# A two-layer graph network on one core: part of the gathered rows fetched by other engines than GpSimd, and nodes normalised once

## What is computed

```python
edge_index = jnp.stack([src, dst])
h = jnp.maximum(_layernorm(x, axis=-1), 0.0)
# layer 0
agg = jax.ops.segment_sum(h[src], dst, num_segments=N_NODES)
x = x + (agg @ W_rel.T + b_rel + h @ W_root.T)
h = jnp.maximum(_layernorm(x, axis=-1), 0.0)
# layer 1
edge_weights = jax.nn.silu(edge_features @ We1 + be1) @ We2 + be2
agg = jax.ops.segment_sum(h[src] * edge_weights, dst, num_segments=N_NODES)
out = jax.nn.silu(agg @ Wn1 + bn1) @ Wn2 + bn2
x = x + (h + out)
```

## Time and profile before

| | us |
|---|---|
| median of 3 runs | 5621.94 (5613.85 to 5627.18) |
| profiled execution, first to last instruction (span) | 3996.3 |
| POOL busy | 2976.2 (74% of the span) |
| PE matmul busy | 2447.1 |
| DVE busy | 1995.0 |
| ACT busy | 1187.2 |

### The profile page before, as it was taken

One profiled execution on the slowest core, in us unless ns is written; L12 is line 12 of the kernel. 1 busy time (PEld: TensorE's weight loads), 2 busy tenths in 40 slices (PEclk: granted clock), 3 DMA queues, 4 the chain that ended last, 5 costly groups with the idle time before them and its releaser, 6 DMA issues.

```text
span 3996.3 us, 52113 instructions
## 1 busy us (share of the span) xinstructions
PE 2447.1 (61%) x10946; PEld 1882.0 (47%) x10946; DVE 1995.0 (50%) x6931; ACT 1187.2 (30%) x2730; POOL 2976.2 (74%) x3135
## 2 busy tenths in 40 slices
PE   3444444444444444444467788877887777887787
PEld 2334333333433333433445555555555555555555
DVE  6555555555555555555554444444444444444444
ACT  3444444444444444444411111111111111111111
POOL 7777777777777777777567777777777777777776
PEclk8555555555555555555578788788788887888878
DMA  2222222222222222222122222222222222222222
GB/s 84 62 61 61 61 64 67 61 61 61 61 64 67 61 61 61 61 66 64 50 78 78 83 80 79 81 76 83 78 80 82 77 75 83 80 79 82 77 76 82
DMA packets 208083, 284.73 MB, mean 71 GB/s; under 512 B 70338, under 2 KB 137972, under 8 KB 207828
## 3 DMA queue, kind: packets, MB, share of 16 engines
q0 software_dynamic: 100096, 205.20, 18.1%
q1 hardware_dynamic: 66676, 58.00, 4.9%
q10 hardware_dynamic: 41184, 20.45, 1.7%
HBM read 262.97 MB, written 20.45 MB: 71 GB/s over the span
## 4 chain that ended last, share of the span: by engine, by line
POOL 67%; issue 23%; PE 5%; DMA 2%; DVE 1%; POOLq 1%; ACT 0%; SPq 0%; DVEq 0%; ACTq 0%
POOL rows L298 67%; PE hid_ps L368 2%; PE seg_a L330 1%; PE ew_ps L373 1%; DMA rows<-h_rows,idx 1%; PE seg_b L330 1%; DMA ef<-ef_blocks 1%; POOLq L176 1%; POOLq L177 0%; DVE rows L670 0%; DVE onehot L566 0%; DVE ew_ps L666 0%; ACT hidden L502 0%; PE node_t L382 0%; ACT rows L436 0%
## 5 line engine op out<-in xcount | busy, mean ns | idle before, releaser
L298 POOL DMA_INDIRECT rows<-h_rows,idx x1564 | 1490.0, 953 | 522.6 <-issue 515.6
L298 POOL DMA_INDIRECT rows<-x,idx x1564 | 1485.2, 950 | 478.2 <-issue 478.2
L330 PE MATMUL seg_a<-onehot,rows 128*128 128x128 f32 x3312 | 726.6, 388 | 915.0 <-DVE onehot L566 408.1
L330 PEld LDWEIGHTS seg_a<-onehot,rows 128*128 128x128 f32 x3312 | 623.7, 281 | 1148.5 <-issue 960.0
L330 PE MATMUL seg_b<-onehot,rows 128*128 128x128 f32 x2944 | 606.4, 370 | 530.9 <-DVE onehot L566 374.4
L424 ACT ACTIVATE rows<-rows,e_shift,e_rstd 128x128 f32<-128x128 f32 x1564 | 643.3, 481 | 793.0 <-DVE e_shift L593 793.0
L330 PEld LDWEIGHTS seg_b<-onehot,rows 128*128 128x128 f32 x2944 | 520.8, 266 | 727.6 <-issue 448.3
L502 ACT ACTIVATE hidden<-hid_ps,be_col 128x512 f32<-128x512 f32 x391 | 268.8, 687 | 1416.1 <-PE hid_ps L368 1415.8
L373 PE MATMUL ew_ps<-we_sb,hidden 128*128 128x128 f32 x3128 | 539.8, 330 | 49.1 <-ACT hidden L502 49.1
L582 DVE BATCH_NORM_STATS2 e_stats<-rows 128x6 f32<-128x128 f32 x1564 | 339.7, 280 | 426.1 <-DMA rows<-x,idx 361.8
L368 PE MATMUL hid_ps<-ef,we_sb 50*128 50x512 f32 x782 | 522.7, 753 | 39.4 <-DMA ef<-ef_blocks 39.4
(11 more groups left out here) (91 smaller groups left out, 811.5 us busy)
## 6 DMA issues: line engine op xcount, KB each, us to landing
ef<-ef_blocks SPq DMA_DIRECT2D x391, 100.0 KB
rows<-x,idx POOLq DMA_INDIRECT x1564, 2.5
rows<-h_rows,idx POOLq DMA_INDIRECT x1564, 2.5
xs<-x SPq DMA_DIRECT2D x26, 256.0 KB
y_rows<-ys ACTq DMA_DIRECT2D x26, 256.0 KB, 2.5
ys<-y_rows SPq DMA_DIRECT2D x26, 256.0 KB, 3.3
out<-xs ACTq DMA_DIRECT2D x26, 256.0 KB
h_rows<-h1s ACTq DMA_DIRECT2D x24, 256.0 KB, 2.5
```

The costliest lines, as they stand in the source:

```text
L298: pool.indirect_dma_start(out=rows[:, u, t, :], out_offset=None, in_=table, in_offset=bass.IndirectOffsetOnAxis(ap=idx[:, j:j + 1], axis=0 ...
L330: mm = pe.matmul(seg[u % 2][:, 0:P], rows[:, u, t, :], onehot[:, u % 2, t, :], start=(t == 0), stop=(t == TB - 1))
```

## The change

**Nodes once.** Ahead of the edges, the 25 groups of nodes are normalised by a loop of five sets at a time (SP loads `x`, DVE statistics, ACT root and scaling, SP stores to a new `h_rows`). PE transposes each and DVE or ACT (`H_BY_ACT`) copies it into a feature-major table in SBUF: `h_table`, which takes the place of `agg1` while layer 0 runs. POOL does its first iteration from `x` as before, all 68 tiles, and these are normalised by block as before. For iterations 1 to 22 it gathers from `h_rows`; statistics, roots and scaling of edges, and `hs` and its transposes in the node updates, are gone from them. SP's weight loads come earlier.

**Tiles by columns.** In these 22 iterations POOL gathers 62 tiles. Of the other six, three come by ACT and two by DVE: for each edge, one instruction copies the 128x1 column of its source node from the table (`columns`), at a place given by a register. Sixteen row numbers at a time are loaded into registers from `cp_idx` (`indices`). PE transposes the finished 128 columns, and ACT copies them into `rows` (`rows_turned`). The sixth tile comes by 128 transfers of one row each, issued by SP (`bring_rows`). In layer 1 it is four tiles of 68, two by ACT, one by DVE, one by SP, in all 23 iterations; its table `h1_table` (in place of `agg0`) is built between the layers, from `h1_rows`, with loads, transposes and copies of 25 groups. The tiles concerned are the last of an iteration: in layer 0 the last two of block 15 and all of block 16, in layer 1 block 16.

The diff, cut to its core:

```diff
+H_SETS = 5
+assert GROUPS % H_SETS == 0
+CHUNK = 16
+CHUNKS = P // CHUNK
+H_BY_ACT = (3, 4)
+CP_ACT = (3, 2)
+CP_DVE = (2, 1)
+CP_TILES = CP_ACT[0] + CP_DVE[0] + 1
+CP_FIRST = U * TB - CP_TILES
...
+        cp_idx = sb("cp_idx", [ITERS, CP_TILES * P], I32)
+        act_cols, dve_cols = sb("act_cols", [P, 3 * P]), sb("dve_cols", [P, 2 * P])
...
+        h_table, h1_table = agg[1], agg[0]
...
+        def indices(engine, it, first, count):
+
+            row = bass.at_runtime_partition(cp_idx[0:1, first:first + count], it)
+            _, values = nc.values_load_multi_w_load_instructions(
+                row, engines=[engine], min_val=0, max_val=N_NODES - 1,
+                skip_runtime_bounds_check_because="edge sources are node numbers")
+            return values
 
...
+            def load_h(k, r):
+                sp.dma_start(h_x[r], node_group(x, k * H_SETS + r)).then_inc(s_hx[r], 16)
+
+            def store_h(k, r):
+                hold(sp, s_hh, k * H_SETS + (r + 1))
+                sp.dma_start(node_group(h_rows, k * H_SETS + r), h_out[r]).then_inc(s_hstore[r], 16)
+
+            for r in range(H_SETS):
...
+            def bring_rows(table, it, first, count):
+                for n, v in enumerate(indices(mybir.EngineType.SP, it, (CP_TILES - 1) * P + first, count)):
+                    r = first + n
+                    sp.dma_start(rows[r:r + 1, U - 1, TB - 1, :], table[bass.ds(v, 1), :]
+                                 ).then_inc(s_sp_row[r // CHUNK], 16)
...
+                with sp.Fori(1, ITERS) as it:
                     i = p * ITERS + it
                     node_x([loop_group(it)], i)
...
+                    hold(sp, s_seg[0], slot_free(i, U - 1, U))
+                    for c in range(CHUNKS):
+                        bring_rows(h_rows, it, c * CHUNK, CHUNK)
+                        if c == CHUNKS // 2:
+                            rows_landed(0, p, it, 0, HALF)
+                            load_idx(it + 1, 0, HALF, s_idx_a)
+                    rows_landed(0, p, it, HALF, U)
                     load_idx(it + 1, HALF, U, s_idx_b)
+                    tile_brought(0, cp_count(0, p, it))
...
+            ROWS_AT, STEP_ROWS = 4, 10
...
+                        if u == ROWS_AT:
+                            hold(sp, s_seg[1], slot_free(i, U - 1, U))
+                        if u >= ROWS_AT:
+                            first = (u - ROWS_AT) * STEP_ROWS
+                            bring_rows(h1_rows, it, first, min(STEP_ROWS, P - first))
                         if u == HALF + 2:
-                            for v in range(HALF):
-                                hold(sp, s_rows[1][v], i * (16 * TB) + 16 * TB)
+                            rows_landed(1, p, it, 0, HALF)
                             load_idx(it + 1, 0, HALF, s_idx_a)
-                    for v in range(HALF, U):
-                        hold(sp, s_rows[1][v], i * (16 * TB) + 16 * TB)
+                    rows_landed(1, p, it, HALF, U)
                     load_idx(it + 1, HALF, U, s_idx_b)
+                    tile_brought(1, tiles0 + cp_count(1, p, it))
...
+                    for j in range(u * TB, min(u * TB + TB, tiles)):
                         pool.indirect_dma_start(
-                            out=rows[:, u, t, :], out_offset=None, in_=table,
+                            out=rows[:, u, j - u * TB, :], out_offset=None, in_=table,
                             in_offset=bass.IndirectOffsetOnAxis(ap=idx[:, j:j + 1], axis=0),
-                        ).then_inc(s_rows[layer][u], 16)
...
-                    gather(0, x, p * ITERS + it, 0)
+                gather(0, x, p * ITERS, p * ITERS, U * TB, first=True)
+                for r in range(H_SETS):
+                    hold(pool, s_hstore[r], 16 * (GROUPS // H_SETS + 1))
+                with pool.Fori(1, ITERS) as it:
+                    i = p * ITERS + it
+                    gather(0, h_rows, i, i, CP_FIRST)
...
+                    gather(1, h1_rows, i, passes * ITERS + i, (U - 1) * TB)
...
+            def turn_act(layer, n, k):
+                if k == 0:
+                    pe.wait_ge(s_cp_rows[layer], n + 1)
+                pe.wait_ge(s_cp_act[layer], n * CP_ACT[layer] + (k + 1))
+                pe.transpose(cp_ps[:, k * P:(k + 1) * P], act_cols[:, k * P:(k + 1) * P],
+                             ident[:, :]).then_inc(s_act_turn[layer], 1)
+
+            def turn_dve(layer, n, k):
+                out = node_t[0][:, k * P:(k + 1) * P] if layer == 0 else cp_ps[:, CP_ACT[1] * P:(CP_ACT[1] + 1) * P]
+                pe.wait_ge(s_cp_dve[layer], n * CP_DVE[layer] + (k + 1))
...
+                        if u == 6:
+                            turn_act(0, n, 0)
+                        if u == 11:
+                            turn_act(0, n, 1)
+                            turn_dve(0, n, 0)
+                        if u == U - 2:
+                            turn_act(0, n, 2)
+                            turn_dve(0, n, 1)
...
+                        if u < U - 2:
+                            pe.wait_ge(s_rows[0][u], i * (16 * TB) + 16 * TB)
+                        elif u == U - 2:
+                            pe.wait_ge(s_rows[0][u], n * 32 + 32)
+                            pe.wait_ge(s_cp_rows[0], n + 2)
+                        else:
+                            pe.wait_ge(s_sp_tile[0], n + 1)
...
+                        if u == 8:
+                            turn_act(1, i, 0)
+                        if u == U - 2:
+                            turn_act(1, i, 1)
+                            turn_dve(1, i, 0)
...
+                def relu_h(r):
+                    act.wait_ge(s_hshift, k * H_SETS + (r + 1))
+                    act.wait_ge(s_hcopy[r], k + 1)
+                    act.wait_ge(s_hstore[r], k * 16 + 16)
+                    for t in range(TB):
+                        op = nc.scalar.activation(h_out[r][:, t, :], h_x[r][:, t, :], ACT.Relu,
+                                                  bias=e_shift[:, r, t:t + 1], scale=e_rstd[:, r, t:t + 1])
...
+            def columns(layer, table, n, it, c):
+                k, q = c // CHUNKS, c % CHUNKS
+                if q == 0:
+                    act.wait_ge(s_act_turn[layer], n * CP_ACT[layer] + (k + 1))
+                tile = (0, CP_TILES - TB)[layer] + k
+                for e, v in enumerate(indices(mybir.EngineType.Activation, it, tile * P + q * CHUNK, CHUNK)):
+                    at = k * P + q * CHUNK + e
+                    op = nc.scalar.activation(act_cols[:, at:at + 1], table[:, bass.ds(v, 1)], ACT.Copy)
+                if q == CHUNKS - 1:
...
+            def rows_turned(layer, n, i):
+                act.wait_ge(s_act_turn[layer], n * CP_ACT[layer] + 2 * CP_ACT[layer])
+                act.wait_ge(s_dve_turn[layer], n * CP_DVE[layer] + 2 * CP_DVE[layer])
+                act.wait_ge(s_seg[layer], slot_free(i, U - 1, U))
+                if layer == 0:
+                    nc.scalar.activation(rows[:, U - 2, 2:4, :].rearrange("p t f -> p (t f)"),
+                                         cp_ps[:, 0:2 * P], ACT.Copy)
+                    nc.scalar.activation(rows[:, U - 1, 0:1, :].rearrange("p t f -> p (t f)"),
+                                         cp_ps[:, 2 * P:3 * P], ACT.Copy)
+                    nc.scalar.activation(rows[:, U - 1, 1:3, :].rearrange("p t f -> p (t f)"),
+                                         node_t[0][:, 0:2 * P], ACT.Copy).then_inc(s_cp_rows[0], 1)
+                else:
...
+                stats_h(0)
+                for r in range(H_SETS):
+                    if r + 1 < H_SETS:
+                        stats_h(r + 1)
+                    shift_of(r, s_hstd, s_hrecip, s_hshift, k * H_SETS + (r + 1))
+                    if r >= 2:
+                        copy_h(r - 2)
...
+            def columns(layer, table, n, it, c):
+                k, q = c // CHUNKS, c % CHUNKS
+                if q == 0:
+                    dve.wait_ge(s_dve_turn[layer], n * CP_DVE[layer] + (k + 1))
+                tile = (CP_ACT[0], CP_TILES - 2)[layer] + k
+                for e, val in enumerate(indices(mybir.EngineType.DVE, it, tile * P + q * CHUNK, CHUNK)):
+                    at = k * P + q * CHUNK + e
+                    op = v.tensor_copy(dve_cols[:, at:at + 1], table[:, bass.ds(val, 1)])
+                if q == CHUNKS - 1:
...
-                        if u + 1 < U:
-                            edge_shift(i, u + 1)
+                        for c in columns_at(0, u):
+                            columns(0, h_table, cp_count(0, p, it), it, c)
...
+            with dve.Fori(0, GROUPS // H_SETS) as k:
+                for r in range(H_SETS):
+                    if r not in H_BY_ACT:
+                        dve.wait_ge(s_tturn, k * H_SETS + (r + 1))
+                        v.tensor_copy(h1_table[:, bass.ds(k * (H_SETS * BLOCK) + r * BLOCK, BLOCK)],
+                                      h_turn[r][:, :]).then_inc(s_tcopy[r], 1)
...
```

(2 more changed lines are left out.)

360 lines of the change are left out of this document (269 added, 91 removed).

## The result

The changed kernel takes 7319.81 us (7311.54 to 7323.74), the kernel before beside it 5624.56: a ratio of 1.302, 95% interval 1.300 to 1.304. The forecast was 5468 us with a range to 5800, and faster: the sign and the size are both wrong.

What follows compares the result with a forecast made beforehand. POOL's gathers, one every 1.25 us, were taken as the bound, with a DVE and PE chain behind. Start +1, layer 0 -143, late updates -9, between layers +20, layer 1 -23 gave -154: 5468 us, range 5200 to 5800.

Steps and rivals of the forecast that it cites:

- The constant of 1625.6 us: Whole kernel: the median's excess over the profiled span of 3996.3 us, taken to stay the same after the change.
- the rival that spread it over the gathers: POOL in both layers: 0.52 us more for each of 3,128 gathers, gain 397, time 5225 us; chance 0.22.
- Cost 1 us: Nodes' stage at the start: POOL waits for slot 0 until about 96; its second iteration began at 95 before.
- The cover named at 60 us: Start: POOL's first iteration of 68 gathers hides the nodes' stage, worth 60 us if it fails.
- The forecast of DVE's chain: Layer 0: DVE needs 77.5 us an iteration, equal to POOL; 78.5 taken, gain 143 us.
- the 0.35 of the author's estimate: Load of 16 row numbers into registers in one instruction: 0.35 us, near one register's 0.30.
- A block of 3.65 us "becomes 5.6": Layer 1, DVE: a group of columns before the multiply adds 1.9 us to its block.
- PE at the slower pace throughout: Layer 1: upper bound of 89 us an iteration, where 83.3 was summed and 84 taken.
- A second term of layer 1: SP's work with row transfers, row number loads and feature loads: 80 us an iteration, POOL's time.
- Each register costs by itself: Register loads on DVE and ACT: 536 us per us of load, a loss from 0.64 us; chance 0.24.
- Column copies shut POOL out: DVE's column copies block POOL's gathers in both layers: about 1100 us over its gain, 6500 us; chance 0.04.
- POOL stays the bound in both layers: If a DVE column costs 0.10 us or less: gain 278, time 5344 us; chance 0.10.

Runs made afterwards that it cites:

- e1_before: The kernel before, unedited, run again for its trace: 5674.51 us, ratio 1.001.
- e12_best: Changed kernel with columns in layer 0 alone (three tiles ACT, one DVE), no SP rows: 5986.75 us, 1.056 of the kernel before.
- e10_l1_act: Changed kernel with SP's tiles of both layers and DVE's tile of layer 1 back on POOL: 6179.62 us, 1.090 of the kernel before.
- e13_after: The changed kernel, unedited, run again where the kernel before takes 3993 us: 4505.75 us, ratio 1.128.
- e14_columns_0: The kernel of e12_best again, where the kernel before takes 3993 us: 3877.73 us, ratio 0.972.
- e15_l1_act: The kernel of e10_l1_act again, where the kernel before takes 3993 us: 3958.24 us, ratio 0.991.
- e18_cols_after: Changed kernel with DVE's columns of layer 1 moved behind the multiplication: 4294.54 us, ratio 1.076 to the kernel before at 3993 us.
- e5_loop_sp: Kernel before plus extra SP waits in a short loop (4 waits, 6 times) in each block: 4001.08 us, ratio 1.000.
- e3_nodes_once: Changed kernel without columns, SP rows or layer 1 table; nodes normalised once, POOL gathers all tiles: 5614.88 us, 0.993 of the kernel before.
- e2_long_sp: Kernel before plus 34 already-satisfied waits on SP, written out in each of 17 blocks: 6171.43 us, ratio 1.090.
- e4_short_bodies: Changed kernel with fewer tiles moved (layer 0: one each by ACT, DVE, SP; layer 1: one by ACT): 6727.01 us, 1.188 of the kernel before.

## Why the prediction was wrong, step by step

**The constant of 1625.6 us.** This is the step that failed first, and it decides the time on chip A. "I take it as constant", and the rival that spread it over the gathers: both are out. The gathers take 0.95 us on either chip. As far as the rows of e1_before and of the changed kernel show, it is time in which the other engines stand still while POOL gathers, and it is longer in the versions that give these more to do (52, 70, 89 and 114 thousand instructions): 1678 us for the kernel before (5671.51 less 3993.27), 2109 for e12_best (5986.75 less 3877.73), 2221 for e10_l1_act (6179.62 less 3958.24), 2867 for the changed kernel (7372.84 less 4505.75). Of its loss of 1701 us on chip A 512 are there on chip B as well; the other 1189 are this growth, whose cause stays open. A difference between the runs and the trace that is 40% of the trace says that the trace is of another case, not that a constant is missing.

**The model against chip B.** There the same steps can be held to the span of 3996.3 us, for which they were made. By the adds of DVE, before and after (e13_after):

```
                                    before   after   change   forecast
start to first add of iteration 1    116.0   171.7    +55.7         +1
layer 0 from there                  1860.5  1835.8    -24.7       -143
between the layers                    55.5    70.5    +14.9        +11
layer 1                             1951.3  2409.5   +458.2        -23
end                                   12.9    11.4     -1.5          0
span                                3996.3  4498.9   +502.6       -154
```

*The start.* "Cost 1 us" held for POOL, whose second iteration starts at 105.5 (forecast 96). But DVE's first add comes at 105, not 38, and its 67 us of backlog are then at the head of the chain that is the bound. The cover named at 60 us does fail, since DVE has no slack to catch up. Where POOL stays slower than DVE it is recovered: e14_columns_0 has iterations of 74 to 76 us until it meets POOL at 80.

*Layer 0.* The forecast of DVE's chain was 77.5 to 78.5 us an iteration; it is 83.9. In the medians from add to add, the 14 blocks with one group and the node update take 64.2 us (4.2 to 4.6 for a plain one) where the terms gave 14 x 4.0 + 4.5 = 60.5; the turn with block 0 takes 10.5 where they gave 6.5 + 2.9 = 9.4; and the last two blocks 9.1 where they gave 2 x 3.2 + 1.2 = 7.6. Block 15 is the longer of these, 5.9: its tiles come by way of ACT, whose loads (L210, 13.9%) and columns (L673, 8.8%) are part of the chain from 250 to 1900 us, though the forecast had ACT 14 us off it. In the group two errors met: a load of 16 registers takes 1.12 us on DVE, not the 0.35 of the author's estimate, but 16 columns take 1.87 us, not 2.08, and part of the load lies under the one-hot. These rows show one of the 66 groups out of 352 that have a pause of 0.33 us inside, for which the profile names no reason, 2.24 us in all:

```profile
1008.03 0.69 DVE L851 TENSOR_TENSOR onehot<-iota_ps,dst_rel 128x512 f32<-128x512 f32 x1
1009.36 1.30 DVE L916 COPY dve_cols<-agg 128x1 f32 x11 [0.64 <-issue]
1010.99 0.61 DVE L916 COPY dve_cols<-agg 128x1 f32 x5 [0.33 <-issue]
```

*Between the layers.* Forecast +11, measured +15: this part held.

*Layer 1.* Here the 458 us are. A block of 3.65 us "becomes 5.6" is the term that was mis-sized: it takes 7.0 to 7.5. DVE and PE in one such block of e13_after:

```profile
3016.49 0.29 DVE L862 TENSOR_TENSOR agg<-seg_a,agg 128x128 f32 x1 [2.34 <-PE seg_a L458]
3016.72 0.69 DVE L851 TENSOR_TENSOR onehot<-iota_ps,dst_rel 128x512 f32<-128x512 f32 x1
3018.06 0.27 DVE L916 COPY dve_cols<-agg 128x1 f32 x2 [0.65 <-issue]
3018.66 1.64 DVE L916 COPY dve_cols<-agg 128x1 f32 x14 [0.33 <-issue]
3020.25 0.70 DVE L978 TENSOR_TENSOR ew_ps<-ew_ps,be_all 128x512 f32<-128x512 f32 x1
3020.99 0.69 DVE L986 TENSOR_TENSOR rows<-ew_ps,rows 128x512 f32<-128x512 f32 x1
3024.01 0.29 DVE L862 TENSOR_TENSOR agg<-seg_b,agg 128x128 f32 x1 [2.34 <-PE seg_b L458]
```
```profile
3004.87 1.15 PE L458 MATMUL seg_a<-onehot,rows 128*128 128x128 f32 x8 [1.75 <-DVE rows L986]
...
3009.21 2.08 PE L541 MATMUL ew_ps<-we_sb,hidden 128*128 128x128 f32 x8 [2.13 <-ACT hidden L750]
...
3014.28 2.07 PE L458 MATMUL seg_a<-onehot,rows 128*128 128x128 f32 x8 [1.00 <-DVE rows L986]
3016.15 1.92 PE L541 MATMUL ew_ps<-we_sb,hidden 128*128 128x128 f32 x8
3017.99 2.07 PE L536 MATMUL hid_ps<-ef,we_sb 50*128 50x512 f32 x2
3021.81 2.07 PE L458 MATMUL seg_b<-onehot,rows 128*128 128x128 f32 x8 [1.75 <-DVE rows L986]
3023.67 1.91 PE L541 MATMUL ew_ps<-we_sb,hidden 128*128 128x128 f32 x8
3025.52 1.40 PE L536 MATMUL hid_ps<-ef,we_sb 50*128 50x512 f32 x2
```

From one add to the next 7.52 us: 0.23 and 1.34 to the end of the register load (0.65 of it not hidden by the one-hot), 2.19 of columns, 1.43 of bias and product, 2.33 for PE's sum. A block without a group in a row of such takes 3.6 with a sum of 1.15. So this group costs 2.2 for its columns (half of layer 1's groups have the pause of 0.33 inside, the others take 1.87), 0.65 for the load and 0.9 because the sum takes 2.07 instead of 1.15 us. PE's granted clock is 0.50 there, against 1.00 before and after (it stands behind POOL's busy time):

```profile
3006.00:3009.00 3.00, 1.07 (x3) 0.24 (x2) 0.29 (x1) 1.82 (x2) 2.39 (x3) 1.00 0.38 110
3009.00:3025.50 16.50, 13.55 (x44) 9.76 (x44) 8.98 (x41) 8.00 (x67) 12.54 (x14) 0.50 0.24 67
3028.00:3032.00 4.00, 2.81 (x18) 1.86 (x16) 2.38 (x16) 2.94 (x18) 2.83 (x4) 1.00 0.27 75
```

It fell at the turn, after pauses of 1.75 and 2.13 us, stayed down through the pauses of 1.00 and 1.75 us ahead of the next two sums, and rose after 3025.5 (0.88 up to 3028, then 1.00), when PE had worked without a pause from 3021.8 on. At that clock PE's own work for a block, from 3014.28 to 3020.06, takes 5.8 us. The blocks without a group are longer too: 3.9 to 5.8 where the forecast had 3.65. Held against the forecast's 83.3 us, the medians below, 105.7 us in sum, have 11 us more in the seven blocks with a group (node update counted), 9 in the nine without and 2 in the turn. The clock was left out of the sum: "PE at the slower pace throughout" stood only in the bound of 89. The windows of layer 1, with the granted clock behind POOL's time, in e13_after and in e15_l1_act, where DVE has no group:

```profile
2090.00:4480.00 2390.00, 1794.82 (x7248) 1306.49 (x7248) 1247.66 (x4504) 923.69 (x6271) 1353.09 (x1435) 0.72 0.23 63
```
```profile
2090.00:3930.00 1840.00, 1504.99 (x7199) 1067.59 (x7198) 889.54 (x1585) 918.44 (x6258) 1390.73 (x1475) 0.84 0.29 81
```

The median time from the add of block 0, 1, ... 16 to the next add shows it by block; DVE's groups stand in blocks 0, 1, 3, 5, 7, 9, 11 and 13, so the first, third and so on to the thirteenth number are those of blocks with a group, and the last is the turn. Node updates lie in these numbers, and SP's waits in those of e18_cols_after:

```
e13_after       7.5 5.0 7.1 5.7 7.5 4.1 7.1 5.8 8.5 4.5 7.1 4.3 7.5 5.7 4.1 3.9 10.4
e18_cols_after  5.9 4.2 6.0 4.6 6.6 4.6 6.3 3.8 7.4 3.7 6.3 3.6 5.8 4.6 6.3 4.6 12.5
e15_l1_act      4.2 3.9 3.6 3.7 3.9 3.6 4.3 5.0 5.5 4.5 4.7 5.0 4.5 5.1 5.0 4.1  9.7
```

A second term of layer 1 was wrong without being felt: SP needs 94.2 us an iteration, not 80. A row transfer took less than forecast, 0.41 us and not 0.47, but the 13 loads of row numbers take 21.9 us and not 5.9. Those of ten numbers take 1.12 to 1.34 us where they start at number 0, 20, 40 and so on, and 2.26 to 2.77 where they start at 10, 30, 50; why is not shown. With DVE's chain as forecast, SP would still have held layer 1 above the 85 us of before, as e18_cols_after shows.

**The rivals.** *Each register costs by itself*: in between. One register takes 0.305 us, sixteen take this (ns min/median/max, e13_after):

```profile
L210 ACTq TENSOR_LOAD <-cp_idx x896: 1010/1029/1575, 159.1 to 4468.2; - x180
L210 DVEq TENSOR_LOAD <-cp_idx x536: 1094/1122/1553, 164.7 to 4466.5; - x179
```

SP's loads of 16 in layer 0 take 1.18. So fifteen registers more cost 0.7 to 0.9 us, though not by a fixed price for each, as SP's loads of ten show. That is beyond the 0.64 us at which the rival turned the sign, and by its 536 us for each us of load it would have given 3842 + 0.77 x 536 = 4255 as the span. Of the other 244 us the start has 55; that the rest is PE's clock is argued from the rows above, not shown by a run. *Column copies shut POOL out*: no, the gathers take 949 ns on average beside them on chip B, 953 before. *POOL stays the bound in both layers*: that is what e14_columns_0 is, with fewer tiles, and there the price of a gather, 1.25 us, is exact.

*Two slips in reading* cost nothing: POOL shows 7 tenths in 37 slices, not 39, and its first 68 gathers end at 95 us, not 89, by the one gather of 6.99 us.

**Open.** What makes the engines of chip A stand still beside unbroken gathers, and why not those of chip B, isn't settled. The gathers' data isn't it: their packets took 12.6 ms in sum on A (e1_before) and 12.0 on B (e5_loop_sp). Code that is fetched in the loop isn't needed for it (e3_nodes_once, layer 1 without an instruction packet from 2800 to 5500 us), but longer bodies came with a longer standstill, by their fetched code or by the number of executed instructions (layer 0 at 123.7 us an iteration in e2_long_sp against 104.4 in e1_before, at 144.6 in e4_short_bodies against 99.7 in e3_nodes_once). These two were not parted, and breaks between the gathers were not tried on chip A.

## What to carry to other kernels

Ahead of any sum, hold the trace's span against the timed runs: where they differ by more than per cents, the trace is of another case, and work moved onto engines that look idle in it may not be idle time at all. Work placed in front of what another engine waits for can cost more than its length: the group of columns above cost 2.2 us for its columns, 0.65 for its load of registers and 0.9 because PE's sum took 2.07 instead of 1.15 us, at a granted clock of 0.50; two tiles on ACT, off that chain, cost nothing in layer 1 on chip B (81.7 us an iteration with 66 tiles on POOL, e15_l1_act). When such a place is tested by moving the work, ask which engine leads the chain afterwards: here it was a third one. And where a late start meets a chain without slack, it stays in the time (55.7 us in e13_after).
